# Second phase of a two-layer kernel: mean square and 1 - a² on ScalarE, the root ahead of both gelus, routed variance on GpSimd, gate and output product in halves

## What is computed

```python
xn = rmsnorm(x, gamma1);  z = xn @ W_in.T;  gate, xc = z[..., :256], z[..., 256:]
xc = causal depthwise conv of 4 taps over tokens (xc) + conv_b
g = xc @ W_gates.T + b_gates;  forget, inp = g[..., :256], g[..., 256:]
alpha = exp(-8 * softplus(forget_base) * sigmoid(forget))
beta = sqrt(1 - alpha**2 + 1e-6)
h = scan over tokens of  h = alpha * h + beta * sigmoid(inp) * xc
x = x + (gelu(gate) * h) @ W_out.T
gz = rmsnorm(x, gamma2) @ W_grow.T;  mgate, mx = gz[..., :256], gz[..., 256:]
return x + (gelu(mgate) * mx) @ W_shrink.T
# expert: softmax over 8 logits, argmax, position in the expert by a running count,
# tokens beyond 100 of an expert dropped, out = gate_probability * (x @ w_expert + b_expert)
```

## Time and profile before

| | |
|---|---|
| median of three runs | 1412.35 us (1409.59 to 1415.34) |
| profiled execution | 1412.17 us |
| its span, first to last instruction | 1410.3 us |
| mean granted TensorE clock | 0.942 |
| busy over the span | TensorE 86%, VectorE 83%, ScalarE 67%, GpSimd 59% |
| steps of the second phase | one about every 27 us from 1002 to 1330 us |

### The profile page before, as it was taken

One profiled execution on the slowest core, in us unless ns is written; L12 is line 12 of the kernel. 1 busy time (PEld: TensorE's weight loads), 2 busy tenths in 40 slices (PEclk: granted clock), 3 DMA queues, 4 the chain that ended last, 5 costly groups with the idle time before them and its releaser, 6 DMA issues.

```text
span 1410.3 us, 26184 instructions
## 1 busy us (share of the span) xinstructions
PE 1216.0 (86%) x8688; PEld 504.3 (36%) x8688; DVE 1164.5 (83%) x2518; ACT 945.8 (67%) x1638; POOL 831.3 (59%) x1068
## 2 busy tenths in 40 slices
PE   1789999999999999999999999558989989989963
PEld 0223333333333333333333323224455545545542
DVE  2868999999999999999998996443898888899764
ACT  1268788878878788787887778445666575665630
POOL 5304636646646746656565465444678787777664
PEclk7589999999999999999999999778999999999976
DMA  1121111111101101101100100000000000000000
GB/s 54 46 82 43 34 37 43 35 36 43 40 30 44 41 28 43 43 28 40 43 31 29 36 12 2 0 0 1 1 16 9 8 8 16 8 8 16 8 8 22
DMA packets 52516, 37.87 MB, mean 27 GB/s; under 512 B 8864, under 2 KB 51744, under 8 KB 52384
## 3 DMA queue, kind: packets, MB, share of 16 engines
q1 hardware_dynamic: 52384, 36.22, 8.0%
HBM read 6.31 MB, written 4.19 MB: 7 GB/s over the span
## 4 chain that ended last, share of the span: by engine, by line
PE 41%; DVE 19%; POOL 14%; issue 13%; ACT 8%; SPq 3%; DMA 0%; POOLq 0%; ACTq 0%; DVEq 0%
PE bank L201 9%; PE bank L182 9%; DVE neg_max L487 8%; PE bank_pair L744 5%; PE bank_pair L169 4%; PE bank L228 3%; SPq L633 3%; PE bank L210 3%; ACT probs L377 2%; PE bank L235 2%; PE bank_pair L804 2%; POOL probs L1173 2%; PE bank L752 1%; DVE y_q L468 1%; POOL x_all L1167 1%
## 5 line engine op out<-in xcount | busy, mean ns | idle before, releaser
L487 DVE TENSOR_REDUCE neg_max<-bank_pair 128x2 f32<-128x1024 f32 x512 | 610.7, 1216 | 87.9 <-PE bank_pair L169 85.8
L377 ACT ACTIVATE probs<-bank 128x512 f32<-128x512 f32 x1024 | 569.3, 598 | 165.4 <-PE bank L182 163.0
L182 PE MATMUL bank<-q_stack,k_stack 50*128 50x512 bf16 x1024 | 352.2, 387 | 30.5 <-ACT probs L377 22.8
L201 PE MATMUL bank<-probs,v_pad 128*32 128x256 f32 x4096 | 331.7, 394 | 0.4 <-issue 0.2
L169 PE MATMUL bank_pair<-k_stack,q_stack 48*128 48x512 bf16 x1024 | 292.0, 395 | 34.4 <-DMA k_stack<-k_parts 18.0
L182 PEld LDWEIGHTS bank<-q_stack,k_stack 50*128 50x128 bf16 x1024 | 79.4, 93 | 274.5 <-ACT probs L377 234.1
L201 PEld LDWEIGHTS bank<-probs,v_pad 128*32 128x32 f32 x4096 | 83.0, 108 | 166.8 <-issue 160.3
L744 PE MATMUL bank_pair<-probs,w_gates 128*128 128x512 f32 x256 | 122.5, 624 | 0.8 <-ACT f_bf L334 0.8
L744 PE MATMUL bank_pair<-probs,w_grow 128*128 128x512 f32 x128 | 75.3, 719 | 32.2 <-ACT probs L909 30.1
L559 POOL TENSOR_SCALAR tiny<-mv_b 128x4 f32<-128x4 f32 x16 | 4.0, 252 | 163.7 <-DVE mv_b L52 163.7
L514 POOL TENSOR_TENSOR q_rest<-q_rest,q_parts 128x512 f32<-128x512 f32 x16 | 20.2, 1266 | 119.3 <-ACT q_rest L323 119.3
(11 more groups left out here) (246 smaller groups left out, 2287.7 us busy)
## 6 DMA issues: line engine op xcount, KB each, us to landing
q_stack<-q_parts SPq DMA_DIRECT2D x384, 32.0 KB
k_stack<-k_parts SPq DMA_DIRECT2D x384, 32.0 KB
x_all<-in_z_dram SPq DMA_DIRECT2D x16, 256.0 KB, 3.1
out_dram<-x_all SPq DMA_DIRECT2D x16, 256.0 KB, 2.3
q_stack<-max_rows SPq DMA_DIRECT2D x64, 8.0 KB
w_gates<-in_w_gates_dram SPq DMA_DIRECT2D x1, 512.0 KB, 3.7
w_in<-in_w_in_dram SPq DMA_DIRECT2D x1, 256.0 KB, 2.7
w_grow<-in_w_grow_dram SPq DMA_DIRECT2D x1, 256.0 KB, 3.9
```

Source lines behind the costliest of these rows:

```text
L182: nc.tensor.matmul(st_ps[h][:, :], k_stack[par][rows, p, c * P:(c + 1) * P], q_stack[par][rows, p, :], start=True, stop=True).then_inc(s[" ...
L201: mm = nc.tensor.matmul(acc[32 * g:32 * g + 32, cols], v_pad[bpar][:, kc, 4 * a + g, :], probs[:, at + g, cols], start=(t == 0 and kc == 0 ...
L377: nc.scalar.activation(probs[:, 4 * (n % RING) + g, :], st_ps[g % 2][:, :], ACT.Exp, scale=SCALE)\
L487: nc.vector.tensor_reduce(neg_max[j // 4][:, c, j % 4, :], score_ps[c % 2][:, :, :], AX_X, ALU.max, negate=True).then_inc(s["max_read"], 1)
```

## The change

Five edits, all in `hawk_moe_phase`. The mean square of h comes from four ScalarE squares with an accumulator output instead of VectorE's statistics. 1 - a² moves from GpSimd to ScalarE (a copy with scale -1 and bias 1). The root follows at once, ahead of the tanh of inp and both gelus; the gelu set is loaded right behind it and the exp set at the end of the step, where also the z3 copies now stand. The variance of the routed output (two products and an addition) moves from VectorE to GpSimd. `gh` is made in two halves, each of which raises its semaphore, and the out product runs over the first half for all chunks, then over the second. On VectorE the x3 statistics move ahead of u.

```diff
 tensor:
-            wait(pe, s["gh_ready"], b + 1)
             wait(pe, s["xh_ready"], b)
-            natural(bank_o, gh, w["out"], s["wout_ps"])
+            for k in range(2):
+                wait(pe, s["gh_ready"], 2 * b + k + 1)
+                for c in range(C):
+                    mm = nc.tensor.matmul(bank_o[:, c * D:(c + 1) * D], gh[:, k, c * P:(c + 1) * P], w["out"][:, k, :],
+                                          start=(k == 0 and c == 0), stop=(k == 1), skip_group_check=True)
+            mm.then_inc(s["wout_ps"], 1)
 scalar, behind alpha:
+        if live(i, -2):
+            b = i - 2
+            wait(act, s["xh_ready"], b + 1)
+            wait(act, s["xn2T_ps"], b)
+            wait(act, s["rs_h_step"], 2 * b)
+            for c in range(C):
+                A(xn2[:, c * D:(c + 1) * D], zx[par][:, c * D:(c + 1) * D], ACT.Square, accum_out=h_sum[:, c:c + 1])\
+                    .then_inc(s["stat_h"], 1)
...
 scalar, behind the xT copy (z3 copies removed here):
+            wait(act, s["sq_ready"], b + 1)
+            A(beta, beta, ACT.Copy, bias=1.0, scale=-1.0).then_inc(s["om_ready"], 1)
+        if live(i, -1):
+            b = i - 1
+            wait(act, s["om_ready"], b + 1)
+            A(beta, beta, ACT.Sqrt, bias=consts["tiny"][:, 0:1]).then_inc(s["beta_ready"], 1)
+        nc.scalar.preload_act_table_set("gelu_and_others")
...
 scalar, behind the convolution copies:
-            wait(act, s["om_ready"], b + 1)
-            A(beta, beta, ACT.Sqrt, bias=consts["tiny"][:, 0:1]).then_inc(s["beta_ready"], 1)
...
 scalar, behind the gelu of gate:
+        nc.scalar.preload_act_table_set("exp_and_others")
+        (the z3 copies of batch i-1, with their three waits)
 vector:
-            wait(dve, s["xh_ready"], b + 1)
-            wait(dve, s["rs_h_step"], 3 * b)
-            raw("h", "h", chunk(zx[par]))
-            aggregate("h", "h", b)
...
-            TT(top[:, 4, :], top[:, 3, :], top[:, 3, :], ALU.mult).then_inc(q, 1)
...
-            TT(top[:, 5, :], top[:, 4, :], stats["y"][1][:, :, 1], ALU.mult).then_inc(q, 1)
...
-            TS(rs["y"][:, 0, :], top[:, 5, :], EPS, None, ALU.add).then_inc(q, 1)
 (count, x3 statistics and their aggregation now stand between the scaled t and u)
 pool:
-            TT(r[:, 0, :], mv[:, :, 0], mv[:, :, 0], ALU.mult).then_inc(q, 1)
-            wait_apart(gp, q, 3 * b + 1, past_wait)
-            TT(r[:, 1, :], r[:, 0, :], mv[:, :, 1], ALU.add).then_inc(q, 1)
+            TS(r[:, 0, :], h_sum[:, :], 1.0 / D, None, ALU.mult).then_inc(q, 1)
...
-            wait_apart(gp, s["sq_ready"], b + 1, past_wait)
-            TS(beta, beta, -1.0, 1.0, ALU.mult, ALU.add).then_inc(s["om_ready"], 1)
...
+            TT(top[:, 4, :], top[:, 3, :], top[:, 3, :], ALU.mult).then_inc(q, 1)
+            wait_apart(gp, q, at + 1, past_wait)
+            wait_apart(gp, s["stat_y"], C * (b + 1), past_wait)
+            TT(top[:, 5, :], top[:, 4, :], stats["y"][1][:, :, 1], ALU.mult).then_inc(q, 1)
+            wait_apart(gp, q, at + 2, past_wait)
+            TS(rs["y"][:, 0, :], top[:, 5, :], EPS, None, ALU.add).then_inc(q, 1)
...
-            TT(gh, h, gate_g[(par + 1) & 1], ALU.mult).then_inc(s["gh_ready"], 1)
+            for n in range(2):
+                TT(gh[:, n, :], h[:, n, :], gate_g[(par + 1) & 1][:, n, :], ALU.mult).then_inc(s["gh_ready"], 1)
```

More of the change, by code:

```diff
@@ L697, in hawk_moe_phase @@
     xc_pad = padded[:, 0:T + TAPS - 1]
-    stats = {n: (sb(f"bn_{n}", [P, C, 6]), sb(f"mv_{n}", [P, C, 2])) for n in ("h", "t", "x3", "y")}
+    stats = {n: (sb(f"bn_{n}", [P, C, 6]), sb(f"mv_{n}", [P, C, 2])) for n in ("t", "x3", "y")}
+    h_sum = sb("h_sum", [P, C])
     stats["x2_0"], stats["x2_1"] = [(sb(f"bn_x2_{k}", [P, C, 6]), sb(f"mv_x2_{k}", [P, C, 2])) for k in range(2)]
@@ L810, in tensor @@
             b = i - 4
-            wait(pe, s["route_step"], 8 * b + 3)
+            wait(pe, s["route_step"], 5 * b + 3)
             wait(pe, s["count_step"], 2 * b)
@@ L844, in scalar @@
             wait(act, s["top_step"], 2 * (b + 1))
-            wait(act, s["route_step"], 8 * b)
+            wait(act, s["route_step"], 5 * b)
             A(exps[:, :, :], shifted[:, :, :], ACT.Exp).then_inc(s["exps_ready"], 1)
@@ L916, in scalar @@
             wait(act, s["gate_ps"], i + 1)
-            wait(act, s["gh_ready"], i - 1)
+            wait(act, s["gh_ready"], 2 * (i - 1))
             A(gate_g[par], pair0[:, :, :], ACT.Gelu).then_inc(s["gate_ready"], 1)
+        nc.scalar.preload_act_table_set("exp_and_others")
+        if live(i, -1):
+            b = i - 1
+            wait(act, s["rs_x2_step"], 5 * (b + 1))
+            wait(act, s["t_ready"], b - 1)
+            wait(act, s["xn2_ready"], b - 1)
+            for c in range(C):
+                A(zx[(par + 1) & 1][:, c * D:(c + 1) * D], x_all[:, b, c * D:(c + 1) * D], ACT.Identity,
+                  bias=rs_x2[(par + 1) & 1][:, 3, c:c + 1], scale=rs_x2[(par + 1) & 1][:, 1, c:c + 1])\
+                    .then_inc(s["z3_ready"], 1)
     def vector(dve, i, par):
@@ L951, in vector @@
             wait(dve, q, 2 * b + 1)
-            wait(dve, s["route_step"], 8 * b)
+            wait(dve, s["route_step"], 5 * b)
             wait(dve, s["exps_ready"], b)
@@ L959, in vector @@
             b = i - 4
-            q, at = s["route_step"], 8 * b
+            q, at = s["route_step"], 5 * b
             wait(dve, s["top_step"], 2 * (b + 1))
@@ L1000, in vector @@
             b = i - 4
-            q, at = s["route_step"], 8 * b
+            q, at = s["route_step"], 5 * b
             wait(dve, q, at + 4)
+            wait(dve, s["rs_y_step"], 5 * b)
             nc.vector.reciprocal(top[:, 3, :], top[:, 2, :]).then_inc(q, 1)
[L1004 to L1007, removed]
-            TT(top[:, 4, :], top[:, 3, :], top[:, 3, :], ALU.mult).then_inc(q, 1)
         if live(i, -3):
@@ L1012, in vector @@
             scaled(t, chunk(t), stats["t"][1], rs["t"][:, 1, :], s["tn_ready"])
+        if live(i, -4):
+            b = i - 4
+            qc, atc = s["count_step"], 2 * b
+            wait(dve, qc, atc)
+            nc.vector.tensor_reduce(counted[:, :], chosen[:, :, :].rearrange("p c e -> p e c"), AX_X, ALU.add)\
+                .then_inc(qc, 1)
+        if live(i, -3):
+            b = i - 3
+            wait(dve, s["x3_ready"], b + 1)
+            raw("x3", "x3", x_chunk(b))
+        if live(i, -3):
+            aggregate("x3", "x3", i - 3)
         if live(i, -1):
@@ L1052, in vector @@
             wait(dve, q, at + 2)
-            wait(dve, s["rs_y_step"], 2 * b)
+            wait(dve, s["rs_y_step"], 5 * b)
             STT(top[:, 7, :], top[:, 6, :], float(CAPACITY), top[:, 3, :], ALU.is_le, ALU.mult).then_inc(q, 1)
@@ L1084, in vector @@
             wait(dve, s["xs_ready"], b + 1)
-            wait(dve, s["gh_ready"], b)
+            wait(dve, s["gh_ready"], 2 * b)
             for n in range(2):
```

41 lines of the change are left out of this document (11 added, 30 removed).

## The result

The kernel after takes 1394.59 us (median of four runs, 1393.75 to 1399.37) against 1413.17 before (median of four runs, one more than in the table above, 1409.59 to 1415.34): a ratio of 0.988, 95% interval 0.985 to 0.991. I had forecast 1404.9. The profiled execution took 1394.3 us with a span of 1392.6, so the traces differ by 17.7 us of span, where I had 7.3. The mean granted clock went from 0.942 to 0.966.

A forecast was written before the change was run, and what follows sets the result against it. The bound was taken to be a loop through several engines (gh, xn, xc, tap 0, scans), no engine being full. From 1412.2: +2.6 steps, -7.2 low-clock stretches, -2.7 end gave 1404.9 us, range 1396 to 1422.

The forecast's parts named there:

- The bound: Steady step: the loop gh, xn, transpose to xc, conv copy, tap 0 to scans sets the whole 26.73 us period.
- Rival D: TensorE before the last grow product: the gelu stall is the bound, 2.38 us come back whole, 1376; chance 0.03.
- steps under 26.5: Sign on step length: 26.9 us was expected, and steps under 26.5 would mean the named loop is wrong.
- The first steps ... none of it ends a wait there: 0: Early steps: two in-line exp loads (1.28 each) go and ScalarE queue comes; effect 0, within 1.5 us.
- The step sum, +0.2: Steady step: +0.12 halves, -0.20 h4's wait, +0.28 later y chain; bounds -0.3 and +0.7; 13 steps make +2.6 us.
- Rival C: VectorE and GpSimd: one collision lands beside ScalarE-bound time before tap 0, step 0.6 shorter, 1397; chance 0.15.
- The squares, 1.64: ScalarE: four accumulating 128x128 squares of h take 1.64 us, between 0.9 and 2.5, leaving slack 0.3 before xc.
- rival A: ScalarE arrives late at the xc copies if the four squares exceed 1.9 us; 1422 us; chance 0.20.
- The clock: Steady part: all four low-clock stretches, 1.8 us each, go because no remaining gap reaches 2.38; -7.2 us.
- Rival B: Low-clock stretches stay or move before the xT transpose, where the 1.7 gap comes; 1412 us; chance 0.17.
- nothing in the steady loop waits for it: gh halves: the out product may begin at half time without steady gain; halves cost +0.12 in the loop.
- The end, -2.7: Last steps: about 1 us gained at gh, -1.9 from halves beside the out product, +0.2 on GpSimd; together -2.7.

The follow-up runs named there:

- experiment 12: Kernel after with GpSimd's z3 power moved from between the halves of xn to behind xn: 1386.55 us, 0.980.
- experiment 1: Kernel after with the root and gelu table load put back behind the convolution copies: 1412.88 us, 0.999 of before.
- experiment 10: Kernel before with unread matmuls in TensorE's stall ahead of the last grow product: 1406.47 us with 8, 1423.51 us with 16.
- Experiment 4: Kernel before with only the early ScalarE root (with 1 - a², loads, z3 copies) and x3 statistics ahead of u: 1393.61 us, 0.985.
- experiment 11: Kernel after with unread 1024-column ScalarE copies ahead of the tanh of inp: 1396.52 us with one, 1429.84 us with two.
- experiment 9: Kernel after with the output product gh whole, in one instruction of 1024 columns: 1404.65 us, 0.994.
- 14: Kernel before with early root, x3 statistics ahead of u and the z3 power behind xn, gh not in halves: 1398.49 us, 0.989.
- experiment 6: Kernel before with early root, x3 statistics ahead of u and gh in halves: 1394.87 us, 0.987.
- experiment 2: Kernel before with only the root, 1 - a², table loads and z3 copies moved on ScalarE: 1413.54 us, 1.000.

## Why the prediction was wrong, by its own steps

**The bound: right.** I had named the loop gh, xn, xT to xc, conv, tap 0, scans. It holds after (the first norm's multiplication still ends TensorE's 1.42 wait, tap 0 still waits for ScalarE, `gh` for the scans), and experiment 12 shortens the step by cutting it, experiment 1 leaves the step alone by undoing the root. Rival D (2.38 us whole) is out for the steady step. One of my signs says otherwise: steps under 26.5 were to mean that the loop is wrong, and they are 26.38. The sign was badly set, as the lower bound of my own step sum (-0.3) already gave 26.43; what failed is the sum below, not the loop.

**"The first steps ... none of it ends a wait there: 0": a step that failed.** Distances 2 and 3 are 5.6 us shorter. Timeline of TensorE before, in those steps:

```profile
972.67 3.56 PE L744 MATMUL bank_pair<-probs,w_grow 128*128 128x512 f32 x4 [2.81 <-ACT probs L909]
...
998.57 1.98 PE L744 MATMUL bank_pair<-probs,w_grow 128*128 128x512 f32 x4 [1.80 <-ACT probs L909]
```

and of GpSimd before, in the same stretch:

```profile
1001.09 2.37 POOL L1173 TENSOR_TENSOR probs<-probs 128x1024 f32<-128x1024 f32 x1 [6.19 <-DVE probs L1087]
```

and of VectorE before, h4 in both steps:

```profile
994.93 1.12 DVE L935 TENSOR_SCALAR probs<-x_all,mv_x,rs_x 128x128 f32<-128x128 f32 x4 [0.93 <-POOL rs_x L1107]
...
1021.24 1.12 DVE L935 TENSOR_SCALAR probs<-x_all,mv_x,rs_x 128x128 f32<-128x128 f32 x4 [0.93 <-POOL rs_x L1107]
```

GpSimd stands 6.19 us before the `gh` at 1001.09, where it stands 2.28 in the steady step: batch i-4 is not there yet, so no y operations collide with the taps and scans ahead of it. The first loop is then shorter, the gelu's is not, and the gelu stall that I had rightly put off the steady path is on the path here. From `gh` to tap 0 it is 19.17 and 18.48 before, and 17.15 and 17.14 after, as in every later step: 3.4 of the 5.6 us. Of these, about 1.6 are the low clock at 972.5 (17.60 in experiment 10, where the stall is filled) and the rest is the stall. The other 2.2 lie between tap 0 and the next `gh`, and 2.0 of them are h4's wait: I had read it as 0.20 in a steady step, and here it is 0.93, so h4 starts 1.0 later behind tap 0 than in the kernel after, twice. Experiment 1 tells the two apart: with the late root `gh` to tap 0 is 19.16 again (and 22.62 with a low-clock stretch in it), while h4 stays early. Experiment 4 keeps the distances at 23.82 and 26.27, so root and order alone do this. I had read one steady step closely and put a bound on the others without reading them.

**The step sum, +0.2: the term that failed most.** It measures -0.34, which is 6.4 us over the whole phase. From the start of `gh` to tap 0: 17.05 before, 17.15 after; I had +0.12 for the halves, they measure 2.50 against 2.36. From tap 0 to the next `gh`: 9.68 before, 9.24 after; I had +0.08 (-0.20 for h4, +0.28 for the y chain). The h4 wait went as said (-0.27). The y subtraction starts 18.14 after the step's start, not 18.8 (17.96 before), and the collisions that it brings are cheaper, not dearer: from tap 1 to the end of the scans it is 7.45 in place of 7.62. The whole term is -0.44 in place of +0.08. Rival C's time, 1397, is close to the measured one, but by luck: its mechanism, a collision that lands ahead of tap 0, did not occur. The collisions are still in the loop, moved from the state input to the scans, and cost 0.17 less together.

**The squares, 1.64: mis-sized.** They take 1.17. By that, ScalarE's slack is 0.91 and not 0.3; experiment 11 measures it to a few hundredths. It changed no time, only rival A's chance. The estimate of 0.9 us worked out from the Trainium skill, "ScalarE: Activation LUTs", section "What ACT_TABLE_LOAD costs", was the nearer one, and its slack of 1.0 too; the page's drain of 1380 ns does not show in this trace either: the tanh starts 0.01 us after the end of the 1.28 us load (rows at 1088.50 and 1089.80).

**The clock: right.** All four stretches of the steady part are gone. Three fell in full steps and cost 5.7 there (1.9 each, I had 1.8); the fourth, at 1324, stands at the last distance and cost about 0.6 there (experiment 10), so 6.3 for the four. What I did not count is a fifth, at 972.5 in an early step. The one at 1328.8 after belongs to the end: it stands 10 us ahead of the last `gh`, as that of 1347.9 stands 8 ahead of it before. Rival B's stretches did not move to the new wait of 1.42. But my reason for the halves ("nothing in the steady loop waits for it") was wrong: no step of the loop waits for the second half, but TensorE's wait in front of the out product is 0.77 with and 1.89 without, and the clock hangs on that (experiments 9 and 14).

**The end, -2.7: -2.3 with the fourth stretch in it, so about -1.7 without.** The halves' part was right (-1.9 said, -2.0 in experiment 6), and it is all there is: the 0.8 us that I had for the other parts do not show.

In sum, 10.4 us of the change in span were missed: 6.4 by the step sum, 5.2 by the early steps and 0.7 by an earlier start of the phase; clock and end gave 1.5 and 0.4 less than I had.

## What to carry to other kernels

Read a pipelined loop at its filling and draining too: a stall that is covered in the steady step by another loop can be the bound where that other loop's stage is not yet live. An edit that shortens one wait may be worth nothing until the queue behind the next one is put in order, so test parts in pairs, not only alone: here root and order are 0 and 0 alone and 20 us together. And where the granted clock drops behind a long wait, count not only how long TensorE waits but in how many pieces: the same kernel with the same work differs by 10 us by that.

## What the runs showed of the hardware

- A 128x128 Square with accumulator output is two rows, 0.30 for the operation and 0.19 to read the accumulator, and four follow each other at 0.29 us.
- A low clock can settle into a steady pipeline: 27.23 per step in nine steps in a row against 26.30 at full clock (experiment 9), 30.66 in five against 27.62 (11), with one low-clock stretch in each. In the kernels with low-clock stretches in the steady part TensorE's longest wait in one piece in the step was 1.89, 1.97, 2.07, 2.35, 2.38 or 2.48; in the others it was 1.42 or less, and 1.76 once. A long wait is not enough by itself: experiment 2 has 2.38 before the out product in each step, and only three low-clock stretches in the steady part; in experiment 11 the steps of 27.6 had one of 1.97 at full clock. What decides between these was not settled.
- Filling a wait with matmuls that nothing reads made the kernel faster by 7.6 us (experiment 10).
- A 128x4 product beside GpSimd took 1.23 us on VectorE; on GpSimd the same operation takes 0.20 in the median. Timeline group of its line, kernel after (shortest, median, longest in ns):

```profile
L1157 POOL TENSOR_TENSOR top<-top,mv_y x16: 200/203/732, 1014.9 to 1383.9; 128x4 f32<-128x4 f32 x16
```
